# A DLRM forward pass on one core: SP and ACT fetch the last embedding column of twelve tiles instead of ten, and their row numbers lie one tile to a partition

## What is computed

```python
h = relu(dense @ dw1 + db1)
dense_emb = relu(h @ dw2 + db2)
sparse_emb = emb_tables[f_ids, sparse_idx]            # B x 26 rows of 64 floats
emb = concatenate([dense_emb[:, None, :], sparse_emb], axis=1)      # B x 27 x 64
inter = einsum('bfd,bgd->bfg', emb, emb)
pairs = inter[:, iu0, iu1]                            # 351 products of two different rows
z = concatenate([emb.reshape(B, -1), pairs], axis=1)
z = relu(z @ ow1 + ob1)                               # 512 wide
z = relu(z @ ow2 + ob2)                               # 256
z = relu(z @ ow3 + ob3)                               # 128
return z @ ow4 + ob4                                  # 1
```

## Time and profile before

| | us |
|---|---|
| median of 3 runs | 532.12 (531.58 to 532.66) |
| the profiled execution, its own time | 532.47 |
| its span, first to last instruction | 530.4 |
| outside the span | 2.1 |
| PE busy | 446.7 (84%) |
| POOL busy | 385.6 (73%) |
| DVE busy | 155.2 (29%) |
| ACT busy | 150.1 (28%) |

### The profile page before, as it was taken

How to read it: one execution, slowest core, us unless ns; L and a number is a source line. 1 busy time by engine, 2 the same in 40 slices (tenths; PEclk the granted TensorE clock), 3 DMA queues, 4 the chain that set the end, 5 groups by cost and what they waited for, 6 DMA issues and landing times.

```text
span 530.4 us, 8428 instructions
## 1 busy us (share of the span) xinstructions
PE 446.7 (84%) x2262; PEld 237.3 (45%) x2262; DVE 155.2 (29%) x297; ACT 150.1 (28%) x337; POOL 385.6 (73%) x410
## 2 busy tenths in 40 slices
PE   5958968687786979988696997988979899998998
PEld 1325424353442534444352443535334354535687
DVE  2311503323141321423332132331422323251342
ACT  2403213231241312423231241323223231422442
POOL 5777777777777777777777777777777777777740
PEclk9998989889797997999899797999897899999999
DMA  8321131111111111111111111111111111111110
GB/s 266 112 46 27 29 80 27 28 27 28 29 27 29 27 29 30 26 30 27 29 30 26 28 28 29 29 27 31 26 28 29 25 29 25 28 27 25 29 22 3
DMA packets 19429, 19.56 MB, mean 37 GB/s; under 512 B 9760, under 2 KB 10787, under 8 KB 19369
## 3 DMA queue, kind: packets, MB, share of 16 engines
q0 software_dynamic: 12992, 13.33, 11.5%
q1 hardware_dynamic: 5202, 5.26, 3.2%
q10 hardware_dynamic: 1188, 0.44, 0.4%
HBM read 18.99 MB, written 0.01 MB: 36 GB/s over the span
## 4 chain that ended last, share of the span: by engine, by line
POOL 53%; PE 23%; issue 19%; DMA 3%; DVE 1%; ACT 1%; POOLq 0%
POOL emb L292 52%; PE l_ps L759 7%; PE gram_ps L738 3%; PE l_ps L767 3%; DMA emb<-table_dram,rows 2%; PE tr_ps L791 1%; PE l_ps L854 1%; PE gram_ps L854 1%; POOL own L292 1%; PE tr_ps L700 1%; PE gram_ps L791 1%; PE l_ps L750 1%; PE l_ps L774 1%; ACT h L533 1%; DVE pairs L352 1%
## 5 line engine op out<-in xcount | busy, mean ns | idle before, releaser
L292 POOL DMA_INDIRECT emb<-table_dram,rows x396 | 375.9, 949 | 123.8 <-issue 119.4
L759 PE MATMUL l_ps<-w_sb,feat 128*128 128x512 f32 x390 | 202.4, 668 | 3.7 <-ACT feat L496 2.7
L759 PEld LDWEIGHTS l_ps<-w_sb,feat 128*128 128x128 f32 x390 | 80.1, 216 | 107.5 <-issue 100.0
L371 DVE COPY gram_c<-gram_ps 32x432 f32<-32x432 f32 x60 | 36.6, 610 | 150.8 <-PE gram_ps L738 150.4
L700 PE MATMUL tr_ps<-ident_sb,emb 128*128 128x128 f32 x194 | 35.7, 308 | 51.3 <-DMA emb<-table_dram,rows 50.3
L738 PEld LDWEIGHTS gram_ps<-slots 64*128 64x128 f32 x960 | 58.5, 195 | 15.8 <-issue 13.4
L738 PE MATMUL gram_ps<-slots 64*128 64x108 f32 x960 | 63.9, 285 | 1.3 <-DVE gram_c L371 1.3
L700 PEld LDWEIGHTS tr_ps<-ident_sb,emb 128*128 128x128 f32 x194 | 25.0, 154 | 82.3 <-issue 68.1
L516 ACT COPY gram_c<-gram_ps 32x432 f32<-32x432 f32 x60 | 30.5, 509 | 104.9 <-PE gram_ps L738 104.3
L338 DVE COPY feat<-tr_ps 128x512 f32<-128x512 f32 (+1 forms) x32 | 15.7, 492 | 141.1 <-PE tr_ps L700 141.0
L496 ACT COPY feat<-tr_ps 128x512 f32<-128x512 f32 (+1 forms) x32 | 18.5, 577 | 128.8 <-PE tr_ps L700 128.0
(11 more groups left out here) (114 smaller groups left out, 219.9 us busy)
## 6 DMA issues: line engine op xcount, KB each, us to landing
own<-table_dram SPq DMA_DIRECT2D x896, 0.2 KB
emb<-table_dram,rows POOLq DMA_INDIRECT x396, 2.5
own<-table_dram ACTq DMA_DIRECT2D x384, 0.2 KB
w_sb<-ow_dram SPq DMA_DIRECT2D x3, 1024.0 KB, 8.9
w1p_sb<-ow_pairs_dram SPq DMA_DIRECT2D x1, 708.0 KB
w_sb<-ow_dram SPq DMA_DIRECT2D x1, 512.0 KB
w_sb<-ow_dram SPq DMA_DIRECT2D x1, 256.0 KB, 11.8
idx_raw<-idx_dram ACTq DMA_DIRECT2D x1, 208.0 KB, 6.6
```

Of the source, the lines that this page charges most:

```text
L292: pool.indirect_dma_start(out=pair_of(t, c // 2)[:, c % 2 * D:(c % 2 + 1) * D], out_offset=None, in_=table, in_offset=bass.IndirectOffsetO ...
L371: last = nc.vector.tensor_copy(dst, src)
L759: nc.tensor.matmul(l1_ps[t % 2][:], feat[t % 2][:, n - 1, :], w1_sb[:, n - 1, :], start=False, stop=False)
```

## The change

SP's tiles become nine: 2, 4, 5, 7, 9, 10, 12, 13, 15 (before 2, 5, 7, 9, 11, 13, 15). ACT's stay three, 6, 11, 14 (before 6, 10, 14). In all, twelve tiles in place of ten have their last column fetched; the new ones are tiles 4 and 12, while tiles 10 and 11 change hands. POOL issues 404 gathers in place of 406, SP 1152 fetches of a row in place of 896, ACT 384 as before.

The row numbers of the fetched columns lie in 12 partitions of 128 numbers in place of one partition of 1280. The four DVE instructions on them are the same, on the new shape. `own` grows by two tiles, 1 KB in each partition.

```diff
-SP_OWN = [2, 5, 7, 9, 11, 13, 15]
+SP_OWN = [2, 4, 5, 7, 9, 10, 12, 13, 15]
 HELD = 32
-ACT_OWN = [6, 10, 14]
+ACT_OWN = [6, 11, 14]
...
         own = sb("own", [P, len(OWN), 2 * D])
-        own_raw = sb("own_raw", [1, len(OWN) * P], I32)
-        own_f = sb("own_f", [1, len(OWN) * P])
-        own_at = sb("own_at", [1, len(OWN) * P], U32)
+        own_raw = sb("own_raw", [len(OWN), P], I32)
+        own_f = sb("own_f", [len(OWN), P])
+        own_at = sb("own_at", [len(OWN), P], U32)
...
         def fetch(eng, engine_type, a, b):
             _, at = nc.values_load_multi_w_load_instructions(
-                own_at[0:1, a:b], engines=(engine_type,), min_val=0, max_val=(table.shape[0] - 1) * 4 * D,
+                own_at[a // P:a // P + 1, a % P:(b - 1) % P + 1], engines=(engine_type,), min_val=0, max_val=(table.shape[0] - 1) * 4 * D,
                 skip_runtime_bounds_check_because="DVE has clamped the rows")
...
-        "own_idx_dram": _np.concatenate([idx[:, t, NF - 1] for t in OWN])[None],
+        "own_idx_dram": _np.stack([idx[:, t, NF - 1] for t in OWN]),
```

## The result

The changed kernel took **527.74 us** (median of 6 runs, 527.69 to 528.45) where the kernel before took 532.07 (6 runs, 531.30 to 532.66): ratio 0.9922, 95% interval 0.9909 to 0.9935, 4.3 us faster. On two other chips it was 0.9924 (0.9912 to 0.9937) and 0.9925 (0.9912 to 0.9938). So the question of the experiments is where 1.2 us more came from. A part needs no experiment: the time outside the span was 2.0 to 2.1 us in every run of the kernel before for which it is known, and 1.8 to 1.9 in the changed kernel. These 0.2 us of the gain had no term in the forecast, and no run tells where they come from.

The account below looks back on a forecast made before the run. POOL, issuing gathers without a pause, was taken to bound the kernel, with PE following. 2.5 + 0.7 - 0.1 = 3.1 us less gave 529.0 us against the median, chance 72%; range 528.3 to 530.9.

Parts of the forecast that it names:

- SP's rows: SP's 256 more fetches, 0.397 us each, stay hidden; tile 13 ends at 429 us, tile 15 at 480.
- POOL's undisturbed 1.252 us: POOL's step from gather to gather, 0.949 + 0.303 us, carried over unchanged from the kernel before.
- the remainder of 0.2 us beside DVE: Loss of POOL's gathers beside DVE's shortened row-number instructions; 0.2 us kept, between nothing and 0.35.
- the gather near 10 us: Gather at 10.09 beside two 390-column DVE instructions: 1.30 us against 0.949, a 0.35 us loss; no gain forecast there.
- Two gathers less: POOL saves one gather in tile 4 and one in tile 12, each 1.252 us, 2.50 together.
- DVE's four instructions: Row-number instructions at the start shrink to 0.3 us each, so POOL regains 0.7 us, ends 0.55 and 0.90.
- a gather waits out what is left of one instruction: Shared-port rule for POOL beside DVE: a gather waits at most 0.3 us, the sum within 0.1 us of the same.
- SP beside POOL between 378 and 480: SP's added DMAs slow the landing of gathers; 0.1 us lost at tile 14, ends 0 and 0.4.
- The end behind the last gather: The end hangs on tile 15's column 24, with 2.4 us from its gather's start to landing.
- The clock takes part of it back: Rival: PE, early from tile 12, waits and runs a half-clock stretch after 461; 530.7 or 532.4 us, chance 13%.
- SP comes too late: Rival: SP's rows take over 0.417 us each and delay PE at tile 13; 542 us at 0.43, chance 4%.
- PE is the bound: Rival: PE's own work sets the time from tile 12 on; gain only 1.95 us, 530.2 us, chance 6%.

Follow-up runs that it names:

- before, again: The kernel before, unchanged, run once more for a second profile; 533.46 us in a single run.
- numbers later: The kernel before with the DMA of the row numbers moved behind the pair weights on SP's queue; 532.35 us.
- numbers first: The kernel before with the DMA of the row numbers ahead of the four big weight loads, still one partition; 532.50 us.
- layout alone: The kernel before with row numbers in ten partitions and the old ten tiles; 531.65 us, on another chip again 530.89 us.
- layout, padded: Row numbers in ten partitions, the old ten tiles, plus an unused tensor that keeps later tensors at the kernel before's addresses; 532.59 us.
- 12 in place of 13: Row numbers in ten partitions, ten tiles, SP fetching tile 12 instead of tile 13; 530.64 against 532.07 us for the kernel before.
- tiles alone: The kernel before with the new twelve tiles, row numbers still in one partition, 1536 long; 531.07 against 532.61 us.
- without tile 4: The changed kernel without its new fetch in tile 4, so eleven tiles; 529.92 us, 0.9958 of the kernel before.
- without tile 12: The changed kernel without its new fetch in tile 12, so eleven tiles; 529.56 us, 0.9955 of the kernel before.
- changed, again: The changed kernel, unedited, run again beside the kernel before on one chip; 528.12 against 532.34 us.
- changed, third: The changed kernel, unedited, run a third time beside a kernel with thirteen fetched tiles; 527.87 us, 0.9925 of the kernel before.
- four left out: The changed kernel with four columns of tiles 8, 9 and 11 never gathered, so 400 gathers; 523.45 us, 0.9837 of the kernel before.
- thirteen, pieces of 8: The changed kernel plus tile 8 on ACT, the missing rows as eight pieces of 8 in tiles 1 to 8; 527.54 us, 0.9915 of the kernel before.
- The two slower kernels with thirteen tiles: The changed kernel plus tile 8 on ACT: four 16-row pieces at each of ACT's first two places, 552.81 us; or 27 pieces of 19 rows, 556.68 us.

## Why the prediction was off

The table puts the quantities together from the profiles (us; landing is the last gather's, from its start; the last column is the end of the span less the last gather's start):

| kernel | last gather | (12, 2) | span | landing | end behind it |
|---|---|---|---|---|---|
| before | 511.7 | 418.0 | 530.4 | 2.4 | 18.7 |
| before, again | 511.5 | 417.7 | 531.4 | 3.6 | 19.9 |
| numbers later | 511.6 | 418.0 | 530.3 | 2.4 | 18.7 |
| numbers first | 510.8 | 417.3 | 530.5 | 3.3 | 19.7 |
| layout alone | 509.3 | 415.7 | 528.0 | 2.4 | 18.7 |
| layout alone, again | 509.6 | 416.0 | 530.0 | 4.0 | 20.4 |
| layout, padded | 509.8 | 416.3 | 530.5 | 4.4 | 20.7 |
| 12 in place of 13 | 509.9 | 416.2 | 528.7 | 2.4 | 18.9 |
| tiles alone | 510.3 | 417.8 | 529.8 | 3.1 | 19.5 |
| without tile 4 | 508.5 | 416.1 | 527.1 | 2.3 | 18.6 |
| without tile 12 | 508.4 | 414.8 | 527.2 | 2.4 | 18.8 |
| changed | 507.2 | 414.8 | 525.9 | 2.4 | 18.7 |
| changed, again | 507.3 | 415.0 | 526.0 | 2.4 | 18.7 |
| changed, third | 506.9 | 414.4 | 525.7 | 2.5 | 18.8 |
| four left out | 502.2 | 409.9 | 521.2 | 2.4 | 19.0 |
| thirteen, pieces of 8 | 506.0 | 414.5 | 525.7 | 2.4 | 19.7 |

**Right.** POOL set the end and PE came along: the end is never less than 18.6 us behind the last gather's start, and four columns fewer brought 4.7 of 5.0 us. The two gathers bring their steps. SP's rows ended at 479.8 (forecast 480) and its tile 13 at 428.9 (429), partly by luck: SP began 3.2 us earlier than forecast, at 19.2, and needed 0.400 us for a row in place of 0.397. No register load was slower from another partition. No wait shows DVE's later work, the output stores or ACT's new tile in the way. The tail from (14, 0) was 68.6 us at full clock, forecast 69.

**Wrong, all in one direction: the terms of POOL's time.** The step of the prediction that failed is the one that carries POOL's undisturbed 1.252 us from gather to gather over unchanged, without a term or a bound for it (measured: 2 ns less in each of 403, 0.8 us); the smaller misses are the remainder of 0.2 us beside DVE and the gather near 10 us. Between the first and the last gather POOL took 4.61 us less, where "2.5 + 0.7" was forecast:

- *Two gathers less*: 2.50, as forecast.
- *DVE's four instructions*, 0.7 forecast: 0.88 measured (0.90 lost before, 0.02 after). The remainder of 0.2 that I kept was read from the gather at 10.09, beside instructions of 0.6 us; beside those of 0.2 to 0.3 us the profiles with one partition for each tile show 0 to 0.10. With twelve tiles in one partition the loss is 2.1 us, so at its new size the layout is worth more than at the old one. On POOL's side the whole took 4.4 us off (changed again against before again) and the two parts alone 2.2 and 1.2. In time the whole is worth 4.2 to 4.3 us and the parts 1.0 and 1.5; the further difference lies behind the last gather, see below. The sentence of the prediction by which a gather waits out what is left of one instruction was too narrow as well: the gather of 2.46 us waited for two.
- *The undisturbed step*: taken as the same, and it fell from 1.251 to 1.249 us (the gather itself from 947 to 944 ns by the median, with 305 between two in both). 2 ns a step over 403 steps are 0.8 us. It is the largest part of the miss, and its cause stays open.
- *The gather near 10 us*: taken as the same, 0.35 us shorter in the first profile, 0.08 in the second, 0.35 in the third. It changes with when the indices land.
- *SP beside POOL between 378 and 480*: 0.1 of loss forecast; hardly any seen. (14, 0) in the changed kernel started 2.55 us behind its column's gather in the first profile, and 2.44 and 2.38 in the other two, against 2.37 before.

2.50 + 0.88 + 0.8 + 0.35 = 4.5, against 4.6 measured. This is the account of two profiles. By the medians the gain is 4.2 to 4.4 us on three chips, and 0.2 of it lies outside the span, so there the terms of POOL have 4.0 to 4.2 us to explain.

**The end behind the last gather.** The prediction let the end hang on the last gather with 2.4 us to landing, and gave the landing no bound. In eleven of these sixteen profiles it did land within 2.3 to 2.5 us. In the five others it took 3.1 to 4.4 us, PE waited for it, and the end came later by about as much: in all five the end is 16.3 to 16.4 us behind the landing. In each of the five, a packet of 16 KB of instructions began 1.0 to 2.4 us behind the last gather's start; in none of the eleven did one, for there it began at least 1.3 us ahead of that start. The two slower kernels with thirteen tiles fit (3.4 us with the packet at 1.4 us, 2.4 without one until 3.4 us). The other gathers show the same: of 169 read between 390 and 512 us in the first profiles of the kernel before and the changed one, nine landed after 2.9 to 3.3 us, each with such a packet beginning 0.8 to 1.6 us behind its start, and the rest within 2.7. No kernel was built to move the packet, so this is seen and not tested. What decides on which side of the last gather it falls stays open too; from (14, 0) it is 47 to 48 us in the eleven and 51 to 52 in the five. In those five profiles the end lies 0.8 to 2.0 us above 18.7, and no profile of the changed kernel has a late landing.

**The rivals.** "The clock takes part of it back" looked at the right place, and nothing of it came true in three profiles of the changed kernel. Where a kernel was above its floor, a half-clock stretch at tile 12 is not the whole reason: PE was late at (14, 0) by 0.1 to 0.8 us in the five profiles above, but it then waited for the last gather. Only with the thirteenth tile was PE's lateness, 1.0 us, what set the end. Why the layout alone passes on only 0.8 to 1.0 of its 2.1 us can be told for its two profiles, 530.08 us with a landing in time and 532.04 us with a late one, and not for the runs between them; the part of tile 12 in it is not shown. "SP comes too late" and "PE is the bound" fell; the second would have been right one gather further: with thirteen tiles PE took back what POOL gained.

**The range** was made of the ends of the terms that I had. Of the 1.2 us that were missing, the step taken as fixed carries 0.8 and the time outside the span 0.2; the collision near 10 us carries 0.35 in one pair of profiles and 0.08 in another, which is luck.

## What to carry over

Where one engine repeats a step some 400 times without a pause, its mean step belongs in the forecast with an error bar of its own: a few ns are a microsecond, and every hold-up at the start, even one of 0.3 us by another engine's instruction, is paid at the end in full. Where the end hangs on one DMA, look at its landing in several profiles before you put a late end down to the engine that waited. Instructions that feed a side path should be laid out over partitions, not along one, since it is their length that the busy engine meets. And work that is given to an engine as a filler has to fit the gap where it stands: 16 rows did, 19 cost more than twenty microseconds, 8 in another gap were free.

## What the runs showed of the hardware

**How DVE holds a gather.** The slow gathers in these profiles fit one of two patterns or both, except the first of each run, which takes 1.07 to 1.08 us with no DVE instruction beside it. If a tensor_scalar or a scalar_tensor_tensor already runs when the gather starts, the gather ends 0.81 to 0.84 us after that instruction: 17.03 and 17.84, 20.23 and 21.06, 10.56 and 11.39 in the kernel before; 16.49 and 17.31 in the changed one; 15.25 and 16.08 with the numbers first. If a tensor_scalar is already running when the gather comes to its last part, the gather ends 0.12 to 0.13 us after it: 19.38 and 19.51 before, 19.08 and 19.20 with the tiles alone, 14.41 and 14.54 with the numbers first. A scalar_tensor_tensor doesn't do that: the gather of 16.69 ended at 17.84 in the midst of one that ran from 17.06 to 18.54. Both together make the 2.46 us.

It matters who comes first. In the kernel before, a tensor_scalar began at 16.06, 0.33 us before the gather of 15.44 ended: that gather ended in time at 16.39 after 0.95 us, and it was the instruction that took longer, 0.97 us where the same one takes 0.81 with the numbers first. A memset didn't hold a gather (one ran at 11.60 to 11.93, and the gather of 11.69 took 0.95).

The Trainium skill (SBUF — State Buffer, Who interferes with whom) says that a VectorE instruction with two SBUF inputs contends with a GpSimd instruction that reads SBUF and not with one that only writes it, that one in a two-port mode contends with GpSimd, and that whoever issues first has the shared ports for its whole instruction. The patterns agree with that if a gather reads at its start and writes near its end, and if these tensor_scalar run in a two-port mode; neither is shown by itself. In the changed kernel an instruction is 0.2 to 0.3 us long, so there is little left to wait for.

**The 2 ns.** The median step was 1.251 us in three profiles (the kernel before twice, the tiles alone) and 1.249 to 1.250 in all others. The three have in common that the row numbers go to one partition by a DMA between the first-layer weights and the pair weights; with that DMA elsewhere, or to ten to thirteen partitions, it was 1.249, and with the later tensors at their old addresses too. By what means a DMA at 6 us sets the pace of gathers 500 us later stays open.
